# FFN per 1024 tokens after attention for all tokens: gate/up as 2x2 blocks in seven products, h through DRAM, down in eight PSUM banks

## The reference

```python
x = x + jnp.tanh(g_xattn[0]) * _L0_xattn_ref(_layernorm(x, axis=-1), ctx_4096, ctx_4096, L0_xattn_Wq, L0_xattn_Wk, L0_xattn_Wv, L0_xattn_Wo)
x = x + jnp.tanh(g_ffn[0]) * _L0_ffn_ref(_layernorm(x, axis=-1), L0_ffn_W_gate, L0_ffn_W_up, L0_ffn_W_down)
```

## Time and profile before

| what | value |
|---|---|
| median of 3 runs | 2206.23 us (2205.82 to 2207.63) |
| span of the profiled execution | 2204.9 us |
| PE busy, matmuls | 2132.5 us (97%), 10208 |
| DVE busy | 1305.4 us (59%) |
| ACT busy | 833.9 us (38%) |
| POOL busy | 199.7 us (9%) |
| HBM read, written | 203.42 MB, 8.39 MB |

### The profile page before, as it was taken

How to read it: one execution, slowest core, us unless ns; L and a number is a source line. 1 busy time by engine, 2 the same in 40 slices (tenths; PEclk the granted TensorE clock), 3 DMA queues, 4 the chain that set the end, 5 groups by cost and what they waited for, 6 DMA issues and landing times.

```text
span 2204.9 us, 29793 instructions
## 1 busy us (share of the span) xinstructions
PE 2132.5 (97%) x10208; PEld 1777.2 (81%) x10208; DVE 1305.4 (59%) x2171; ACT 833.9 (38%) x1956; POOL 199.7 (9%) x215
## 2 busy tenths in 40 slices
PE   7899999999899999999989999999999898999999
PEld 6788888888688888888868888888887787888887
DVE  6886544456687654445568764444558865445444
ACT  4773322222386333222237633322225753222321
POOL 1330000000033000000013300000001320000000
PEclk9999999999999999999999999999999999999999
DMA  5113522223212353222231234322223122223321
GB/s 181 58 58 116 191 86 86 86 88 103 106 49 77 115 172 102 88 86 86 86 107 48 77 136 151 106 91 88 86 77 125 39 87 95 86 86 114 114 78 56
DMA packets 58909, 213.22 MB, mean 97 GB/s; under 512 B 6448, under 2 KB 6448, under 8 KB 58800
## 3 DMA queue, kind: packets, MB, share of 16 engines
q1 hardware_dynamic: 58800, 211.84, 28.7%
HBM read 203.42 MB, written 8.39 MB: 96 GB/s over the span
## 4 chain that ended last, share of the span: by engine, by line
PE 83%; DVE 9%; ACT 3%; issue 3%; DMA 1%; SPq 0%; POOL 0%; ACTq 0%; DVEq 0%; POOLq 0%
PE ps L952 27%; PE ps L953 26%; PE ps L954 26%; DVE kb_h L677 2%; ACT pb L459 2%; DVE nmx L692 1%; PE ps L1033 1%; PE ps L992 1%; DVE pt_l L629 1%; DVE kb_l L679 1%; PE ps L983 1%; PE ps L1057 1%; DVE qo_l L629 1%; PE ps L984 1%; DMA x<-in_x 1%
## 5 line engine op out<-in xcount | busy, mean ns | idle before, releaser
L952 PE MATMUL ps<-xt_h,wc_h 128*128 128x512 f32 x1184 | 468.2, 395 | 0.0
L953 PE MATMUL ps<-xt_l,wc_h 128*128 128x512 f32 x1184 | 464.5, 392 | 0.0
L954 PE MATMUL ps<-xt_h,wc_l 128*128 128x512 f32 x1184 | 463.8, 392 | 0.0
L629 DVE TENSOR_TENSOR wr_l<-wr_raw,wr_h 128x1024 fp32r<-128x1024 f32 x112 | 139.7, 1247 | 363.3 <-ACT wr_h L403 363.3
L749 DVE SCALAR_TENSOR_TENSOR x<-ps,tg,x 128x512 f32<-128x512 f32 x352 | 258.5, 749 | 159.1 <-PE ps L954 158.9
L952 PE MATMUL ps<-wr_h,h_h 128*128 128x512 f32 x672 | 264.7, 394 | 0.0
L954 PEld LDWEIGHTS ps<-xt_h,wc_l 128*128 128x128 f32 x1184 | 224.0, 189 | 47.4
L953 PE MATMUL ps<-wr_l,h_h 128*128 128x512 f32 x672 | 261.9, 390 | 0.0
L954 PE MATMUL ps<-wr_h,h_l 128*128 128x512 f32 x672 | 261.8, 390 | 0.0
L952 PEld LDWEIGHTS ps<-xt_h,wc_h 128*128 128x128 f32 x1184 | 224.5, 190 | 43.5
L953 PEld LDWEIGHTS ps<-xt_l,wc_h 128*128 128x128 f32 x1184 | 224.4, 190 | 43.4
(11 more groups left out here) (105 smaller groups left out, 3304.3 us busy)
## 6 DMA issues: line engine op xcount, KB each, us to landing
wc_raw<-in_wc SPq DMA_DIRECT2D x216, 512.0 KB, 4.2
wr_raw<-in_wr SPq DMA_DIRECT2D x112, 512.0 KB, 3.4
x<-in_x SPq DMA_DIRECT2D x5, 2048.0 KB, 8.8
out<-x SPq DMA_DIRECT2D x16, 512.0 KB, 2.7
ct_raw<-in_ctx_t SPq DMA_DIRECT2D x15, 512.0 KB, 5.2
xn<-in_x SPq DMA_DIRECT2D x3, 2048.0 KB, 10.0
wo_raw<-in_wr SPq DMA_DIRECT2D x8, 512.0 KB, 5.0
kv_raw<-in_wc SPq DMA_DIRECT2D x8, 256.0 KB, 5.1
```

The costliest lines, as they stand in the source:

```text
L629: return nc.vector.tensor_tensor(out, whole, hi.bitcast(F32), ALU.subtract)
L952: pe.matmul(out, w_h, m_h, start=first, stop=False)
L953: pe.matmul(out, w_h, m_l, start=False, stop=False)
L954: return pe.matmul(out, w_l, m_h, start=False, stop=last)
```

## The change

Attention runs for all 16 batches first, group after group; each group's x1 is stored to DRAM (`x1d`). Between two groups PE makes K and V of the next one and, among them, transposes its normalised x (`xt1`), and DVE takes that x's statistics and splits the first four Q tiles.

Then the FFN runs twice (`s`), for 1024 tokens each time:

- **Token stage.** x1 is read back, two batches for each `t`, and normalised. Tokens form two halves of 512 and the contraction two halves of 512. DVE makes four sums of these blocks (`token_sums`), PE transposes seven blocks for each `t` (28 groups of four), ACT and DVE split each from PSUM into `xop_h` and `xop_l`.
- **Gate/up.** For each of 21 tiles of F (a quad) the 2x2 blocks of weights (gate and up by the halves of the contraction) are combined in four sums on POOL (`weight_sums`) and multiplied in seven products of 4 x 3 matmuls with 512 columns, in place of eight. DVE adds parts of the results (L1076 to L1092), ACT takes silu, POOL multiplies (`hidden`), and SP stores h to DRAM (`hd`). The last 64 rows (`mixed`) are four products.
- **Down.** For each 512 tokens (`p`), h and the rows of the down weights are loaded, split and multiplied step by step in a ring of three; eight PSUM banks hold the sums of all 22 steps. One addition for each bank follows at the end (`add_ffn`). The weights' low part of the 64-row tile is filled with zeros to 128 rows.

The diff, cut to the new FFN; the attention functions keep their instructions:

```diff
+            def load_fraw(s, c, i):
+                par = c % 2
+                if c < 2 and s == 0:
+                    sp.wait_ge(wc_used, NG * NQ)
+                elif c < 2:
+                    sp.wait_ge(y_done, 2 * YN * s)
+                else:
+                    sp.wait_ge(w_lo, splits(s, c - 2, i, PROD))
+                if c == QUADS:
+                    sp.dma_start(fraw[:, par, 0, :], wm[:, :]).then_inc(fraw_in[par], 16)
+                else:
+                    src = wf[c] if isinstance(i, int) else wf[bass.ds(i * 2 + c, 1), :, :].rearrange("o p n -> (o p) n")
+                    sp.dma_start(fraw[:, par, :, :].rearrange("p a n -> p (a n)"), src).then_inc(fraw_in[par], 16)
...
+            def store_h(s, c, i):
+                sp.wait_ge(h_ready, twos(s, c, i, 2))
+                if c == QUADS:
+                    sp.dma_start(hd[s][c, 0:FR, :], hb[0:FR, :, :].rearrange("p a n -> p (a n)")).then_inc(h_out, 16)
...
+            def down(s):
+                sp.wait_ge(w_lo, SPLITS * (s + 1))
+                store_h(s, QUADS, 0)
+                sp.wait_ge(p_done, PRODS * (s + 1))
+                sp.wait_ge(h_out, 16 * FT * (s + 1) + 1)
+                for f in range(STEP0):
+                    load_down(s, 0, f, 0)
+                for p in range(2):
+                    tok = 8 * s + 4 * p
+                    with sp.Fori(0, 6) as i:
+                        for f in range(STEP0, STEP0 + 3):
+                            load_down(s, p, f, i)
+                    load_down(s, p, FT - 1, 0)
+                    if s + p > 0:
+                        sp.wait_ge(stored, 16 * NB * (2 * s + p))
+                    sp.dma_start(xo[:, :, :], x1d[tok:tok + NB].rearrange("t p n -> p t n")).then_inc(xo_in, 16)
+                    if p == 0:
+                        for f in range(STEP0):
+                            load_down(s, 1, f, 0)
+                    for t in range(NB):
+                        sp.wait_ge(y_free, 8 * (2 * s + p) + 2 * t + 2)
+                        sp.dma_start(out[tok + t], xo[:, t, :]).then_inc(stored, 16)
...
+            def weight_sums(s, c, i):
+                par = c % 2
+                pool.wait_ge(fraw_in[par], raw_arrived(s, c, i))
+                if c > 0:
+                    pool.wait_ge(w_lo, splits(s, c - 1, i, PROD - 1))
+                elif s > 0:
+                    pool.wait_ge(w_lo, SPLITS * s)
+                a11, a12 = fraw[:, par, 0, 0:HALF], fraw[:, par, 0, HALF:D]
+                a21, a22 = fraw[:, par, 1, 0:HALF], fraw[:, par, 1, HALF:D]
+                nc.gpsimd.tensor_tensor(fs[:, 0, :], a21, a22, ALU.add).then_inc(fs_ready, 1)
+                pool.wait_ge(fs_ready, sums_made(s, c, i, 1))
+                nc.gpsimd.tensor_tensor(fs[:, 1, :], fs[:, 0, :], a11, ALU.subtract).then_inc(fs_ready, 1)
+                nc.gpsimd.tensor_tensor(fs[:, 2, :], a11, a21, ALU.subtract).then_inc(fs_ready, 1)
+                pool.wait_ge(fs_ready, sums_made(s, c, i, 2))
+                nc.gpsimd.tensor_tensor(fs[:, 3, :], a12, fs[:, 1, :], ALU.subtract).then_inc(fs_ready, 1)
...
+            def hidden(s, c, i):
+                pool.wait_ge(silu, twos(s, c, i, 2))
+                pool.wait_ge(comb, combs(s, c, i, 3))
+                nc.gpsimd.tensor_tensor(hb[:, 1, :], hb[:, 1, :], cc[:, 1, :], ALU.mult).then_inc(h_ready, 1)
+                pool.wait_ge(comb, combs(s, c, i, 5))
+                nc.gpsimd.tensor_tensor(hb[:, 0, :], hb[:, 0, :], cc[:, 0, :], ALU.mult).then_inc(h_ready, 1)
 
...
+            def quad(s, c, i):
+                bx, bz = 3 * (c % 2), 3 * (c % 2) + 2
+                act.wait_ge(p_done, prods(s, c, i, 1))
+                act.wait_ge(comb, combs(s, c, i, 0))
+                copy(x1c[:, :], ps[:, bx, :]).then_inc(x1c_ready, 1)
+                follow = (lambda j: weight_hi(s, c + 1, i, j)) if c + 1 < QUADS else (
+                    lambda j: weight_hi(s, c + 1, i, j) if j in (0, 3) else None)
+                follow(0)
+                follow(1)
+                follow(2)
+                act.wait_ge(p_done, prods(s, c, i, 4))
+                act.wait_ge(h_out, ones(s, c, i) * 16 + 1)
+                nc.scalar.activation(hb[:, 0, :], ps[:, bx, :], ACT.Silu).then_inc(silu, 1)
+                follow(3)
+                follow(4)
+                follow(5)
+                act.wait_ge(comb, combs(s, c, i, 4))
+                nc.scalar.activation(hb[:, 1, :], hb[:, 1, :], ACT.Silu).then_inc(silu, 1)
+                follow(6)
...
+            def normalise2(s, t):
+                dve.wait_ge(rs2, 1)
+                dve.wait_ge(xs_in[t % 2], 32 * (2 * s + t // 2 + 1))
+                for h in range(2):
+                    b = 8 * s + 4 * h + t
+                    where = xs[:, t % 2, h, :]
+                    nc.vector.tensor_scalar(where, where, mv2[:, b, 0:1], rstd2[:, b:b + 1],
+                                            ALU.subtract, ALU.mult).then_inc(xs_ready, 1)
+            def token_sums(s, t):
+                dve.wait_ge(xs_ready, 8 * s + 2 * t + 2)
+                if t >= 2:
+                    dve.wait_ge(xp_done, 28 * s + 7 * (t - 1))
+                b11, b21 = xs[:, t % 2, 0, 0:HALF], xs[:, t % 2, 0, HALF:D]
+                b12, b22 = xs[:, t % 2, 1, 0:HALF], xs[:, t % 2, 1, HALF:D]
+                made = 16 * s + 4 * t
+                v = ts[t % 2]
+                nc.vector.tensor_tensor(v[:, 0, :], b12, b11, ALU.subtract).then_inc(ts_ready, 1)
+                nc.vector.tensor_tensor(v[:, 2, :], b22, b12, ALU.subtract).then_inc(ts_ready, 1)
+                dve.wait_ge(ts_ready, made + 1)
+                nc.vector.tensor_tensor(v[:, 1, :], b22, v[:, 0, :], ALU.subtract).then_inc(ts_ready, 1)
+                dve.wait_ge(ts_ready, made + 3)
+                nc.vector.tensor_tensor(v[:, 3, :], b21, v[:, 1, :], ALU.subtract).then_inc(ts_ready, 1)
+            def tokens_lo(s, t):
+                for j in range(PROD):
+                    n = PROD * t + j
+                    dve.wait_ge(xp_hi, 28 * s + n + 1)
+                    minus(xop_l[:, j, :, t * P:(t + 1) * P], ps[:, 4 + n % 4, :].rearrange("p (k m) -> p k m", k=KH),
+                          xop_h[:, j, :, t * P:(t + 1) * P]).then_inc(xp_lo, 1)
...
+            def quad(s, c, i):
+                bx = 3 * (c % 2)
+                by, bz = bx + 1, bx + 2
+                follow = (lambda j: weight_lo(s, c + 1, i, j)) if c + 1 < QUADS else (
+                    lambda j: weight_lo(s, c + 1, i, j) if j in (0, 3) else None)
+                dve.wait_ge(x1c_ready, ones(s, c, i) + 1)
+                follow(0)
+                dve.wait_ge(p_done, prods(s, c, i, 2))
+                nc.vector.tensor_tensor(u2[:, :], ps[:, by, :], x1c[:, :], ALU.add).then_inc(comb, 1)
+                follow(1)
+                dve.wait_ge(p_done, prods(s, c, i, 3))
+                nc.vector.tensor_tensor(gg[:, :], ps[:, bz, :], x1c[:, :], ALU.add).then_inc(comb, 1)
+                follow(2)
+                follow(3)
+                dve.wait_ge(p_done, prods(s, c, i, 5))
+                dve.wait_ge(comb, combs(s, c, i, 2))
+                dve.wait_ge(h_ready, twos(s, c, i, 0))
+                nc.vector.tensor_tensor(cc[:, 1, :], ps[:, by, :], gg[:, :], ALU.add).then_inc(comb, 1)
+                follow(4)
+                dve.wait_ge(p_done, prods(s, c, i, 6))
+                dve.wait_ge(h_out, ones(s, c, i) * 16 + 1)
+                nc.vector.tensor_tensor(hb[:, 1, :], ps[:, bz, :], u2[:, :], ALU.add).then_inc(comb, 1)
+                follow(5)
+                dve.wait_ge(p_done, prods(s, c, i, 7))
+                nc.vector.tensor_tensor(cc[:, 0, :], ps[:, by, :], x1c[:, :], ALU.add).then_inc(comb, 1)
+                follow(6)
...
+            def tokens(s):
+                if s == 0:
+                    pe.wait_ge(x1_add, NG * YN)
                 else:
-                    for t in range(NB):
-                        xt2(t)
-                pe.wait_ge(xt2_lo, g * 8 + 8)
-                pe.sem_inc(passed, 1)
-                with pe.Fori(0, LOOPS) as i:
-                    for c in range(4):
-                        gate_up(g, c, i, last)
-                    down(g, 0, i)
-                    down(g, 1, i)
-                for f in range(4 * LOOPS, 4 * LOOPS + 4):
-                    gate_up(g, f, 0, last)
-                down(g, 8, 0)
-                down(g, 9, 0)
...
+            def product(s, c, i, n, jw, jx, bank, first, last):
+                pe.wait_ge(w_lo, splits(s, c, i, (jw if c < QUADS else jw // 3) + 1))
+                for k in range(KH):
+                    ins = three(ps[:, bank, :], w_h[:, jw, k, :], w_l[:, jw, k, :], xop_h[:, jx, k, :], xop_l[:, jx, k, :],
+                                first and k == 0, last and k == KH - 1, not first)
+                ins.then_inc(p_done, 1)
+            def quad(s, c, i):
+                bx = 3 * (c % 2)
+                by, bz = bx + 1, bx + 2
```

(30 more changed lines are left out.)

1098 lines of the change are left out of this document (589 added, 509 removed).

## The result

| what | before | changed |
|---|---|---|
| median of 4 runs | 2206.35 us (2205.82 to 2207.63) | 2236.82 us (2236.12 to 2239.34) |
| ratio to before | 1 | 1.014, 95% interval 1.0123 to 1.0157 |
| span of the profiled execution | 2204.9 us | 2234.6 us |

What follows compares the result with a forecast made beforehand. PE's stream, plus the places where it waits, was taken as the bound. 182.1 us come and 150.4 go, 31.7 more than the 2204.9 span: 2236.6, and with 1.3 between span and median 2238 us; range 2208 to 2280.

Steps and rivals of the forecast that it cites:

- saved in gate/up and down, low clock left out: FFN: 504 fewer gate/up matmuls save 114.4 us, down's 64-row matmul 13.6, one transpose set in three groups 10.2.
- the last group's transposes: Last group: the stretch from 1831.98 to 1844.21 is replaced by the token stage, 12.2 us saved.
- hand-overs: Between attention groups: Q waits for all new xt_l, some 31.5 us after K/V starts instead of 27.1; 13.2 us added.
- scores later: After hand-overs: first scores later after Q, 3.9 us in two loop turns, 5.9 in the last group; 13.7 added.
- token stages: Before each gate/up half: DVE's 37.6 us of plain work plus waits, 53 and 62.5 us; 115.5 added.
- gate/up to down: PE stands still before down for one chain of stores, loads and splits, 14 us each; 28 added.
- low clock and pass change: PE restarts at low clock after four stops, 9.0 us added; waits for banks between down's passes, 1 us added.
- The 13.6 us of the 64-row matmul: Down's last chunk: five matmuls take 1.56 us against 1.13; full 128 rows save 13.6 us over 32 times.
- the lock between DVE and POOL: Token stages: POOL sums hold DVE up, up to 9 us more; with half clock a rival at 2258, chance 0.15.
- The rival built on that rule: Token stages wholly at half clock, 11 us more; with the DVE and POOL lock 2258 us, chance 0.15.
- The uncovered pause in the quads' loops: Gate/up, 18 loop turns: DVE's pause exceeds 8.2 us; at 10 it adds 32, 2270 us; chance 0.15.
- Queues run ahead: Hand-overs and token stages: loads land in time and waits overlap, 52 us less, 2186 us; chance 0.10.

Runs made afterwards that it cites:

- the eighth product: The change with the last product of every quad done twice, the first time into a bank nobody reads: 2351.0 us, ratio 1.0652.
- four slots: The change with four slots for x in the hand-over, and all four normalised and transposed ahead of the last K/V product: 2217.76 us, ratio 1.0047.
- down begins early: The change with the first two down steps loaded and split during the last quad and mixed tile, and bank waits moved: 2199.89 us, ratio 0.9977.
- token stage tight: The change with three x1 slots, earlier pow and second-stage x1 loads, later weight splits, and first-quad products waiting only for their own block: 2198.89 us, ratio 0.9963.
- the kernel before with full rows: The kernel before with all 128 rows in place of 64 in the low weights' matmul of the 64-row tile: 2185.4 us, ratio 0.9908.

## Why the prediction was right

It said 2238 for a measured 2236.82. The direction and the chains that make the kernel slower were as told, but that it came within 1.2 us is luck: two terms were off by 9 us with opposite signs, and the low clock by 6. The terms against the two profiled executions (a stretch runs from the start of its first matmul to 0.227 after the start of its last):

| term | forecast | measured | from |
|---|---|---|---|
| saved in gate/up and down, low clock left out | 138.2 | 139.8 | 1433.1 for four FFNs; now 2 x 410.85 + 237.7 + 237.9, less 4.0 |
| the last group's transposes | 12.2 | 12.2 | |
| hand-overs | 13.2 | 14.4 | 31.90, 31.97 and 31.73 for 27.1 |
| scores later | 13.7 | 4.6 | from Q to the end of O: 2.5, 0.6 and 1.5 more |
| token stages | 115.5 | 125.0 | 58.6 + 66.4 |
| gate/up to down | 28 | 30.0 | 15.0 twice |
| low clock and pass change | 10 | 4.0 | down's 237.8 for 235.8, twice |
| end | 1.7 | 1.5 | 5.5 for 4.0 behind the last matmul |
| first group | none | 2.2 | not foreseen; its attention ends between 197.3 and 200.1 in the changed kernels' profiles |
| sum | +31.7 | +29.7 | |

**Seven products.** Right, and shown by itself: the eighth product gives 114.2 back for 114.4. The 13.6 us of the 64-row matmul are tested on the kernel before. There its four FFNs won 12.3 of it. What that kernel won besides lies behind the loop's turns; the change has no down ahead of a turn, so only the term is its share.

**Hand-over.** The chain through DVE ended after 31.9 us for 31.5, with its cause as stated, the second half of x: with four slots the last hand-over falls to 27.3. The term of 13.2 (14.4 measured) fits this profile and not every other: in the profiles of two other kernels with the same attention (down begins early, token stage tight) Q starts up to 34.6 and 35.8 us after K/V, and the term would be 22.4 and 21.0. In five of their six hand-overs DVE's last normalisation of x takes 3.75 us, once 5.17, in place of 1.11, beside the zeros that POOL writes for the next keys. DVE in the change, then DVE and POOL in the kernel whose down begins early:

```profile
225.44 1.11 DVE L929 TENSOR_SCALAR xn<-xn,mv,rstd 128x1024 f32<-128x1024 f32 x1
...
225.70 3.75 DVE L938 TENSOR_SCALAR xn<-xn,mv,rstd 128x1024 f32<-128x1024 f32 x1
...
226.21 1.81 POOL L518 MEMSET kb_l<- 128x2048 f32 x1
```

In both POOL's first `MEMSET` began 1.24 us before it, so the start doesn't decide; what does, no run shows. The kernels with four slots normalise earlier, and there each takes 0.81 at most.

The step on the scores failed. It added DVE's lateness to a pause of 7.05, and the pause was shorter:

```profile
235.73 1.22 DVE L837 TENSOR_TENSOR wc_l<-wc_raw,wc_h 128x1024 fp32r<-128x1024 f32 x1 [1.53 <-ACT wc_h L582]
240.14 0.21 DVE L884 CAST kb_h<-kc_h 32x128 fp32r<-32x128 f32 x1 [3.19 <-issue]
242.22 0.21 DVE L886 CAST kb_l<-kc_l 32x128 fp32r<-32x128 f32 x1 [1.86 <-issue]
```

3.19 and 1.86 are 5.05. A loop's turn on an engine is then no fixed price: 7.05, 5.05, and 5.03 in the kernel before with full rows. In the two turns the first scores came 2.3 and 1.9 us later after Q for 3.9 forecast. In the last group the 5.9 us did not come at all: PE doesn't wait for the first scores there, which come 2.6 us later after Q (17.6 for 14.97), 2.4 of it for the low clock of the first Q matmuls. That the turn was the cause of the pause is shown, since it went when the loop was written out. PE's own turn, which the prediction kept as a bound "hidden so far", was there at 4 us, hidden under the late tokens.

**Token stage.** The sum of plain work was right: with the waits taken away the first stage took 37.3 us. The 37.6 us of plain work have 3.6 of weight splits in them that PE's first product now hides, and 3.4 for the last batch's addition and statistics come ahead. The waits for two loads were forecast at 6.6 for each stage and measured at 7.3 (3.68 + 3.63) in the first, 7.5 in the second. What was sized wrong is the lock between DVE and POOL, left to a rival at "up to 9": it cost 8.5, shown by moving POOL's sums. The Trainium skill, "SBUF — State Buffer" (Who interferes with whom), says that a GpSimd instruction that reads SBUF and a DVE one with two SBUF inputs shut each other out for their length. Here the trace agrees: the sums went from 0.68 to 1.63 and 1.75. It is not the sums alone: a pair of normalisations, with one tensor input and two columns of scalars, went from 1.53 to 3.42 beside POOL too. The prediction had such a row of its own and priced it at nothing; that was the mistake to learn from, since the row was there.

**The low clock.** Forecast at four stops, 2.7 each, it came at five: three hand-overs (12 matmuls at 0.43 for 0.23, 2.4 each, which the table has in its term on the scores and which in the two turns lies inside the wait for them) and two starts of down (about 1.6 each). The first products after both token stages of this profile ran at the full clock (the third window for the first; 0.23 us apart in the second), though nothing but transposes had run on PE for 58 us. The Trainium skill, "TensorE: Matmul & The Clock Gate" (Part 4), has it that transposes do not count as busy work. This trace does not agree: in the last 9.3 us of the stage the granted clock was 0.74 on average, and 1.00 from 831.0 to 833.3. The rival built on that rule (half clock throughout, 11 us) did not come. The full clock was not certain either: in five of the other kernels' profiles the products behind the second token stage began at the low level, and that half of gate/up took 0.8 to 1.7 us longer than 410.85.

**Gate/up to down** was the chain as told. **The uncovered pause in the quads' loops** did not come: PE has no gap there, and DVE's idle at the turn is 3.88 us, put down to ACT:

```profile
874.40 0.69 DVE L837 TENSOR_TENSOR w_l<-fraw,w_h 128x512 fp32r<-128x512 f32 x1
878.97 1.70 DVE L837 TENSOR_TENSOR w_l<-fraw,w_h 128x512 fp32r<-128x512 f32 x1 [3.88 <-ACT w_h L582]
```

The turn of this short body took less than that; 8.2 was the point from which it would have decided. **Queues run ahead** was wrong for the change as it stands and right for what it could be: with more slots, the queues reordered and attention written out it runs in 2132.5 us, 3.35% under the kernel before and, by the ratios 0.9665 and 0.9908, 2.5% under that kernel with full rows.

What stays open: attention ended up to 13 us apart in profiles that share its code. The long normalisations make 7.9 and 6.7 us of that in the two profiles where it ended last; the rest isn't explained, nor are some 3.5 us that the kernel before with full rows won besides in the attention behind its second turn.
